# Scaling factors of the images worked out by ScalarE, and twelve images scaled by VectorE, in a spectral block on one core

## The reference, cut to what matters

```
h    = groupnorm(x)                         # one "group" is 8 columns wide, 32 groups per row
xa_n = inorm(h)
k, q, v = spec_conv(xa_n, ...)              # only the low 8 x 8 modes
att  = inorm(softmax(q @ k.T) @ v) + h
att_n = inorm(att)
mixed = inorm(spec_conv(att_n, mix_w) + skip_w * att_n)
out  = x + (inorm(mixed) + att)
```

## Time and profile before

| | us |
|---|---|
| median of 3 runs | 747.07 |
| lowest, highest | 746.57, 747.50 |
| profiled execution, its own time | 744.31 |
| its span, first to last instruction | 742.5 |

### The profile page before, as it was taken

The page is one execution under the profiler, slowest core; times in us unless marked ns, Lnnn a source line. Parts: engine busy times, 40 slices in busy tenths (PEclk is TensorE's granted clock), DMA queues, the critical chain, the costliest instruction groups (busy, mean ns, idle before and its releaser), DMA issues.

```text
span 742.5 us, 15088 instructions
## 1 busy us (share of the span) xinstructions
PE 665.9 (90%) x5772; PEld 593.6 (80%) x5772; DVE 494.6 (67%) x1141; ACT 331.9 (45%) x710; POOL 353.7 (48%) x388
## 2 busy tenths in 40 slices
PE   6979898899999998989999999889999989886675
PEld 6979798787888888877888889878888889875553
DVE  2866657577677666578677756667777765656565
ACT  5768232364566613255565614246466542332121
POOL 0000024997930003799960002499990001289994
PEclk9999899998999999999999999999999999999799
DMA  8980000696698600298789800079689830025266
GB/s 268 389 310 2 1 2 2 231 302 232 234 304 294 220 1 1 72 322 278 260 297 298 282 11 1 2 260 317 237 292 304 298 110 1 1 110 203 108 235 254
DMA packets 71687, 136.32 MB, mean 184 GB/s; under 512 B 5376, under 2 KB 5888, under 8 KB 71616
## 3 DMA queue, kind: packets, MB, share of 16 engines
q1 hardware_dynamic: 71616, 135.36, 53.4%
HBM read 68.23 MB, written 67.11 MB: 182 GB/s over the span
## 4 chain that ended last, share of the span: by engine, by line
PE 61%; DVE 19%; POOL 8%; issue 4%; DMA 3%; ACT 3%; SPq 1%; DVEq 0%; ACTq 0%; POOLq 0%
PE psY L291 22%; PE psP L343 17%; PE psT L328 6%; POOL X L633 4%; PE psP L397 4%; PE psP L312 3%; PE psY L312 3%; DVE QP L782 3%; DVE X L677 3%; DVE Y L677 3%; DMA X<-in_x 2%; DVE SQ L677 2%; DMA out<-X 2%; ACT SQ L495 1%; DVE Y L680 1%
## 5 line engine op out<-in xcount | busy, mean ns | idle before, releaser
L633 POOL TENSOR_TENSOR X<-X,ALPHA 128x512 f32<-128x512 f32 x256 | 267.1, 1078 | 2.2
L291 PE MATMUL psY<-FWD,X 128*128 128x128 f32 x2048 | 250.0, 281 | 14.5 <-DMA X<-in_x 8.5
L291 PEld LDWEIGHTS psY<-FWD,X 128*128 128x128 f32 x2048 | 237.6, 194 | 30.3 <-issue 25.6
L677 DVE TENSOR_TENSOR X<-X,psP 128x512 f32<-128x512 f32 x256 | 164.5, 684 | 100.1 <-PE psP L343 97.8
L782 DVE TENSOR_REDUCE QP<-SQ 128x32 f32<-128x512 f32 x256 | 161.8, 679 | 62.2 <-ACT SQ L495 43.5
L343 PE MATMUL psP<-INVW,T 64*128 64x256 f32 x1024 | 151.1, 412 | 33.3 <-DVE X L677 17.1
L611 POOL TENSOR_TENSOR Y<-Y,OMEGA 128x256 f32<-128x256 f32 x32 | 24.8, 776 | 326.6 <-ACT Y L499 326.3
L495 ACT ACTIVATE SQ<-X 128x512 f32<-128x512 f32 x256 | 147.2, 623 | 24.6 <-DVE QP L782 11.4
L343 PEld LDWEIGHTS psP<-INVW,T 64*128 64x128 f32 x1024 | 97.9, 193 | 66.1 <-issue 29.3
L517 ACT ACTIVATE T<-psT,BIA,SCL 128x256 f32<-128x256 f32 x128 | 65.3, 561 | 120.5 <-PE psT L328 110.6
L487 ACT ACTIVATE Y<-psY 128x512 f32<-128x512 f32 x128 | 76.1, 594 | 69.5 <-PE psY L291 65.9
(11 more groups left out here) (168 smaller groups left out, 414.7 us busy)
## 6 DMA issues: line engine op xcount, KB each, us to landing
X<-in_x SPq DMA_DIRECT2D x128, 512.0 KB, 5.5
out<-X SPq DMA_DIRECT2D x128, 512.0 KB, 3.8
INVH<-t_inv_h SPq DMA_DIRECT2D x1, 256.0 KB, 5.0
LW<-in_low_w SPq DMA_DIRECT2D x1, 204.0 KB, 3.7
GWT<-t_w SPq DMA_DIRECT2D x1, 192.0 KB, 5.0
FWD<-t_fwd SPq DMA_DIRECT2D x1, 128.0 KB, 2.1
INVW<-t_inv_w SPq DMA_DIRECT2D x1, 128.0 KB, 4.8
LM<-in_low_mix SPq DMA_DIRECT2D x1, 68.0 KB, 3.2
```

The lines of the kernel that those rows point to most:

```text
L291: last = mm(psY[p % 2][:, (2 * i + c) * 128:(2 * i + c + 1) * 128], X[:, 2 * p + i, a, c * 128:(c + 1) * 128], FWD[:, a, :], start=a == 0, ...
L633: P.tensor_tensor(v, v, al, MUL).then_inc(x_scaled, 1)
L677: return V.tensor_tensor(out, a, b, op)
```

## The change

The factors are no longer made by GpSimd, eight images at once in two operations. ScalarE makes them one image at a time, as one activation on 128 x 32: `r * c2 + 1`, with c2 as its scale and a column of ones as its bias. ALPHA now has 16 slots, one per image, used in turn. Four images' factors (a quad's) are one step, `alphas(b, q)`, with one count of `alpha_made`. Two such steps (AHEAD = 2) stand in ScalarE's queue before the first `keep_t` of the batch; the others stand in `produce`, two quads ahead, behind the `keep_t` of a quad. From the fifth on, a step first waits until GpSimd has scaled the images whose slots it takes.

In batch 3, images 19, 23, 27 and so on to 63 (12 of 64) aren't scaled by GpSimd. ScalarE writes their factors into the free banks psY[0] (six, in quad 2) and psY[1] (six, in quad 8), and VectorE scales each in `finish`, waits for the result, and adds psP.

```diff
+AHEAD = 2
-        ALPHA = sb("ALPHA", [128, 2, 8, GROUPS])
+        ALPHA = sb("ALPHA", [128, 16, GROUPS])
+        def by_vector(b, i):
+            return b == B - 1 and i % 4 == 3 and i >= 16
+
+        def scaled_by_pool(b, n):
+            return 64 * b + n - (max(n // 4 - 4, 0) if b == B - 1 else 0)
@@ ScalarE
+            def alpha(dst, i):
+                return nc.scalar.activation(dst, MR[:, 5, :], ACT.Identity, bias=ONES[:, 0:1],
+                                            scale=C2[:, place(i):place(i) + 1])
+
+            def alphas(b, q):
+                if q in (0, 4 * SPLIT // 2):
+                    act.wait_ge(c2_kept, 2 * b + 1 + (q > 0))
+                if q >= 4:
+                    act.wait_ge(x_scaled, scaled_by_pool(b, 4 * q - 12))
+                for i in range(4 * q, 4 * q + 4):
+                    last = alpha(ALPHA[:, i % 16, :], i)
+                last.then_inc(alpha_made, 1)
+
+            def vector_alphas(b, part):
+                q0, q1 = ((4, 4 * SPLIT // 2), (4 * SPLIT // 2, QUADS))[part]
+                if part == 0:
+                    act.wait_ge(mode_weighted, 8 * b + 8)
+                for q in range(q0, q1):
+                    last = alpha(psY[part][:, GROUPS * (q - q0):GROUPS * (q - q0 + 1)], 4 * q + 3)
+                last.then_inc(vector_alpha, 1)
@@ ScalarE, attend
                 mode_powers(b, SPLIT + 1)
+                for q in range(AHEAD):
+                    alphas(b, q)
                 keep_t(b, 0)
@@ ScalarE, produce
                         keep_t(b, 2 * u + 1)
+                    if u + AHEAD < QUADS:
+                        alphas(b, u + AHEAD)
+                    if not more and u in (2, 4 * SPLIT // 2 - AHEAD):
+                        vector_alphas(b, int(u > 2))
                     if u == 1:
@@ GpSimd
-            def alphas(b, g):
-
-                al = ALPHA[:, g % 2, :, :]
-                P.tensor_tensor(al, over(MR[:, 5, 0:1], [[0, 8], [1, GROUPS]]),
-                                over(C2[:, 8 * g:8 * g + 1], [[1, 8], [0, GROUPS]]), MUL).then_inc(alpha_made, 1)
-                pool.wait_ge(alpha_made, 16 * b + 2 * g + 1)
-                P.tensor_tensor(al, al, over(ONES[:, 0:1], [[0, 8], [0, GROUPS]]), ADD).then_inc(alpha_made, 1)
-                pool.wait_ge(alpha_made, 16 * b + 2 * g + 2)
-                for g in range(NG):
-                    if g in (0, SPLIT):
-                        pool.wait_ge(c2_kept, 2 * b + 1 + (g > 0))
-                    if g >= 2:
-                        pool.wait_ge(x_scaled, 64 * b + 8 * g - 8)
-                    alphas(b, g)
-                    for i in range(8 * g, 8 * g + 8):
-                        if i in behind:
-                            weigh(b, behind[i])
-                            add_products(b, behind[i])
+                for i in range(IMGS):
+                    if i % 4 == 0:
+                        pool.wait_ge(alpha_made, QUADS * b + i // 4 + 1)
+                    if i in behind:
+                        weigh(b, behind[i])
+                        add_products(b, behind[i])
+                    if not by_vector(b, i):
                         scale_x(b, i)
@@ VectorE, finish
-                dve.wait_ge(x_scaled, 64 * b + n + 1)
+                v = Xf[:, n, :]
+                if by_vector(b, n):
+                    part, col = (0, GROUPS * (n // 4 - 4)) if n // 4 < 4 * SPLIT // 2 else (1, GROUPS * (n // 4 - 4 * SPLIT // 2))
+                    dve.wait_ge(vector_alpha, part + 1)
+                    xs = X[:, n, :, :].rearrange("p a (g j) -> p a g j", j=GW)
+                    do(tt(xs, xs, over(psY[part][:, col:col + 1], [[0, HC], [1, GROUPS], [0, GW]]), MUL))
+                    wait_link()
+                else:
+                    dve.wait_ge(x_scaled, scaled_by_pool(b, n) + 1)
                 dve.wait_ge(synth_made, 64 * b + n + 1)
-                v = Xf[:, n, :]
                 tt(v, v, psP[n % 3][:, :], ADD).then_inc(out_made, 1)
```

More of the change, by code:

```diff
@@ L149, in spectral_block @@
         FPH = spare[:, 160:224]
-        af = ALPHA[:, :, :, :].rearrange("p s i g -> p (s i g)")
+        af = ALPHA[:, :, :].rearrange("p i g -> p (i g)")
         pow_of = lambda g: Y[:, 0, 1, 8 * g:8 * g + 4, :]
@@ L225, in spectral_block @@
         alpha_made = sem("alpha_made")
+        vector_alpha = sem("vector_alpha")
         x_scaled = sem("x_scaled")
@@ L618, in add_products @@
                                 w[:, 1, :].rearrange("p (q n) -> p q n", q=2), ADD).then_inc(products, 1)
-            def alphas(b, g):
-                al = ALPHA[:, g % 2, :, :]
-                P.tensor_tensor(al, over(MR[:, 5, 0:1], [[0, 8], [1, GROUPS]]),
-                                over(C2[:, 8 * g:8 * g + 1], [[1, 8], [0, GROUPS]]), MUL).then_inc(alpha_made, 1)
-                pool.wait_ge(alpha_made, 16 * b + 2 * g + 1)
-                P.tensor_tensor(al, al, over(ONES[:, 0:1], [[0, 8], [0, GROUPS]]), ADD).then_inc(alpha_made, 1)
-                pool.wait_ge(alpha_made, 16 * b + 2 * g + 2)
             def scale_x(b, i):
                 v = X[:, i, :, :].rearrange("p a (g j) -> p a g j", j=GW)
-                al = over(ALPHA[:, i // 8 % 2, place(i) % 8, 0:1], [[0, HC], [1, GROUPS], [0, GW]])
+                al = over(ALPHA[:, i % 16, 0:1], [[0, HC], [1, GROUPS], [0, GW]])
                 P.tensor_tensor(v, v, al, MUL).then_inc(x_scaled, 1)
```

## The result

| | us |
|---|---|
| forecast | 751.4 (746.8 to 756.0) |
| kernel after, median of 4 runs | 788.29 (768.35 to 808.73) |
| kernel before, beside it on the same chip | 746.82 (742.38 to 747.5) |
| ratio, after to before | 1.0376, 95% interval 1.0286 to 1.0466 |

Every ratio in this document compares the runs of each kernel that lie within 1.5% of its fastest one, so it can differ from the quotient of the medians: here it rests on 768.35 and 779.85 alone, while the medians of all runs lie 5.6% apart. Either way the change costs far more than the 0.6% that was forecast; only the direction was right. The changed kernel's four runs (768.35, 779.85, 796.72, 808.73) lie about 12 to 17 us apart.

The account below looks back on a forecast made before the run. It took TensorE, ScalarE's evictions and, in places, GpSimd's sum and VectorE's coefficients as bounds. Batch terms +0.15, +1.1, +1.1 and +2.0 gave +4.35: profiled 744.31 to 748.7, timed 751.4 us, range 746.8 to 756.0.

Parts of the forecast that it names:

- the four blocked operations: Second-part coefficients on VectorE, batch 1: each waits for a scaling's end, the last done about 347.8, not 345.9.
- the second factor group: Start of a batch: GpSimd no longer makes these factors, two operations of 0.62 with gaps of 0.07, saving 1.38 us.
- Factors: ScalarE's 128x32 activations, priced from T's 128x256 at 561 ns: 375 ns each, one every 0.275 us.
- Start of a batch: GpSimd's first scaling 1.52 us later, less 1.38 saved; ScalarE's sum and TensorE 0.14 later, taken as +0.15 per batch.
- the sum for the third quad: GpSimd's sum of the last mode group, which ScalarE needs before keeping the third quad's T: 0.14 us later.
- Coefficients: Second part: blocking by scalings delays TensorE's resumption 1.1 us in batches 1 and 2 each; batch 3 gains 0.2.
- the gap: Batch 3: GpSimd runs out of factors at 690.1, so the coefficients lose their last block, ready 690.4 instead of 690.6.
- VectorE's scalings: Batch 3: twelve at 684 ns plus 0.05 wait; eight hidden, three exposed at 0.74 us each, 2.2 in all.
- The rival of the falling clock: TensorE's clock falls after the new stall in batches 1 and 2: 2.0 us each, 753.4 or 755.4; chance 0.27.
- my 4.35 us: Whole forecast increase: batch 0 +0.15, batches 1 and 2 +1.1 each, batch 3 +2.0.
- the bound at T's price: Start of a batch: if factors come 0.46 us apart like T's, the shift is +0.83 per batch.
- the four exposed ones: VectorE's batch 3 scalings not hidden: images 23 (counted in the coefficients), 27, 31 and 63; 0.74 us each.

Follow-up runs that it names:

- x17: Kernel before, with GpSimd's first two factor groups computed together ahead of image 0, so its row runs longer without a pause: 766.78 us against 745.88.
- x7: Changed kernel, with GpSimd waiting for its own last scaling before each of images 9 to 12: 748.9 us against 745.95, ratio 1.0126.
- x11: Changed kernel, VectorE's twelve scalings kept, with GpSimd waiting for its last scaling before every second image and before 9 and 11: 751.28 us, ratio 1.0116.
- x16: Changed kernel, with one GpSimd pause per batch, 1, 4, 8 and 9 operations ahead of the end the product can use: 753.21 us, ratio 1.0113.
- x14: Changed kernel without VectorE's scalings or GpSimd self-waits, ScalarE making the first quad's factors earlier and quad 8's one quad later: 732.6 us, ratio 0.9827.

## Why the prediction was wrong

*The step that failed.* "Now each of the four blocked operations waits for the end of a 1.04 us scaling". I took the earlier trace rows for a rule: a blocked operation pays at most the rest of the scaling under way. They followed it in a kernel in which GpSimd stood still twice in every eight scalings, and x17 shows that it fails there too once those pauses lie 13 operations back. I used the rule at the coefficients, where it held, as pacing keeps GpSimd's rows to four there; and it let me leave the start of each batch out of the sum. I counted the second factor group as 1.38 us saved, "two operations of 0.62 with gaps of 0.07", and did not ask what the gaps did. They were the pauses. The term that is missing, the product shut out in each batch, measured 15.08, 15.07, 0.64 and 13.02 us.

The Trainium skill, SBUF — State Buffer, section "Who interferes with whom", says that the loser of the shared port waits out the other's whole instruction. This case's trace disagrees on the size, and decides: 15.67 us against instructions of 1.08.

*Factors.* Forecast 375 ns and one every 0.275 us. Measured 404 and 0.304 (eight in 2.53 us). An estimate by the figures of the Trainium skill (ScalarE: Activation LUTs, section "What ACT_TABLE_LOAD costs"), 399 ns and 0.306 us, was the better one.

*Start of a batch.* Forecast: the sum for the third quad 0.14 us later. From the sum of group 5 to that of group 7 it is 14.05 us where it was 13.80: +0.25. In batch 1, where the clock is 1.00 in both, TensorE starts the third quad 22.33 us behind the batch's first product where it was 22.05: +0.28, after a stall of 1.87 where it was 2.25. So the term was about twice the 0.15 that I took, and inside its bounds. The product itself comes 0.66 us later (22.18 for 21.52), as TensorE waits 0.31 and 0.34 us for T in the first two quads. Of the 3.4 us in the account's first line, 1.1 lie ahead of batch 0's first product (119.8 and 120.9), and so ahead of everything that was changed, and 1.6 are the lower clock at that start.

*Coefficients.* Of batch 1, the timeline of VectorE and of TensorE:

```profile
378.81 1.84 DVE L703 TENSOR_SCALAR Y<-PAIR,IM 64x32 f32<-64x32 f32 x2
380.57 1.12 DVE L703 TENSOR_SCALAR Y<-EYE,IM 64x64 f32<-64x64 f32 x1
381.74 0.49 DVE L707 SCALAR_TENSOR_TENSOR Y<-Y,IM 64x272 f32<-64x272 f32 x1
```
```profile
381.87 0.46 PE L369 MATMUL psB<-Y,SIDE 64*128 64x96 f32 x2 [1.77 <-DVE IM L1004]
```

Against the earlier trace rows: 1.84 for 0.49, 1.12 for 0.64, then 0.49 for 1.36, and a stall of 1.77 us (forecast 1.6). TensorE's next passes for psP came 7.31 us behind the first PAIR operation where they came 6.27 behind it: +1.04 (forecast 1.1). Right in each piece, except that it waited there for ScalarE's T (0.64 us) and not for VectorE. In batch 3 the gap came as forecast, and a little earlier: the first of these two PAIR operations ends with GpSimd's row (at 739.5), and the other two operations are held by nothing.

```profile
738.69 0.95 DVE L703 TENSOR_SCALAR Y<-PAIR,IM 64x32 f32<-64x32 f32 x2
739.57 0.24 DVE L703 TENSOR_SCALAR Y<-EYE,IM 64x64 f32<-64x64 f32 x1
```

*VectorE's scalings.* 680 ns (forecast 684), and the addition behind each 0.72 us later (0.74). The pairs at the end, one even and one odd, of which the last adds what was forecast:

```profile
785.21 0.69 DVE L700 TENSOR_TENSOR X<-X,psP 128x512 f32<-128x512 f32 x1 [0.76 <-PE psP L351]
785.81 0.68 DVE L700 TENSOR_TENSOR X<-X,psY 128x512 f32<-128x512 f32 x1
...
789.29 0.69 DVE L700 TENSOR_TENSOR X<-X,psP 128x512 f32<-128x512 f32 x1 [0.76 <-PE psP L351]
```

4.08 us for a quad, as before. Batch 3 took 2.3 us more beside the product (forecast 2.0).

*The rival of the falling clock* came true in part, and no run isolates it. Busy times by stretch in the kernel after, behind the coefficients of batches 0, 1 and 2; the columns are the five engines (TensorE, its weight load, VectorE, ScalarE, GpSimd), the granted clock, and the DMA's share and rate:

```profile
191.00:199.00 8.00, 7.74 (x50) 6.08 (x51) 5.94 (x15) 2.61 (x7) 1.90 (x3) 0.79 0.52 182
382.00:390.00 8.00, 7.36 (x61) 6.44 (x62) 6.57 (x15) 3.88 (x10) 2.88 (x3) 1.00 0.51 164
558.00:566.00 8.00, 8.00 (x54) 6.96 (x55) 5.85 (x14) 3.03 (x8) 1.14 (x2) 0.79 0.59 200
```

After the 1.77 us stall of batch 1 it stayed at the 2.4 GHz level throughout; in batch 2 part of the stretch ran at the 1.2 GHz level, where before had 1.00.

*The sum without the product* came out too low. Of the runs in which the product isn't shut out, x7 lies 3.0 us over before between the medians and 1.0126 by its ratio, whose interval holds 1.0058, my 4.35 us; x11 lies 8.7 over (1.0116), and x16 7.3 (1.0113), with a PAIR operation of 2.73 us. The account's rest is 8.3 us, 1.1 of it ahead of the change. So all but x7's median put the rest 3 us or more above what I had. The start explains 0.5 of that, if the other batches are like batch 1; what the remainder is stays open, and the levels of the clock are part of it. That the direction was right owes little to these terms: most of the measured loss is the one that I hadn't seen.

*Slips in the sum*, none of which matters to this: the bound at T's price is +0.88 with the 0.05 us that the other terms have; T is done at 656.63 for 656.52, which is +0.11; VectorE would be behind by 1.03, not 0.95; and a scaling of 1,078 ns would also have made the four exposed ones 0.4 us longer each.

## What to carry to other kernels

When a change takes work or waits off GpSimd, look for what its pauses let through: list VectorE's SBUF-only operations that come during GpSimd's rows, and count GpSimd's operations since it last stood still. In these runs one with at most 9 behind that pause waited for one scaling at most; from 13 on, price it at the rest of the row, and at what holds the row up in turn. Put a wait on GpSimd's own last result there: each costs about 0.1 us, and here four in each batch gave back some 38.

## What the runs showed of the hardware

A blocked VectorE operation can wait through 16 GpSimd instructions (15.67 us), and so can other forms of it: tensor_scalar (15.63), 64 partitions (15.67), and for 9 instructions one of 64x32 (9.15). Operations of one element on each partition (64x1) took 0.20 us inside rows of 16 operations and more (x14, x16), and so weren't held. A pause of GpSimd of 0.08 us ended it (x17), and so did a 0.11 us memset between two scalings (3.30). While it waits, VectorE counts as busy.
